# A gated linear-attention block on one NeuronCore: the decayed queries move from GpSimd to VectorE

## What is computed

```python
# attention branch: q, k, v = silu(causal_conv(xn @ W_qkv)), 8 key heads, 16 value heads of 128
q = _l2norm(repeat(q)) * 128 ** -0.5;  k = _l2norm(repeat(k))
beta = sigmoid(xn @ W_b);  g = -exp(A_log) * softplus(xn @ W_a + dt_bias)
def step(S, inp):                       # over the tokens, state S per head, 128 x 128
    S = S * exp(g_t)
    v_adj = (v_t - k_t @ S) * beta_t
    S = S + outer(k_t, v_adj)
    return S, q_t @ S
s = (rmsnorm(o) * norm_weight * silu(xn @ W_z)) @ W_out
# expert branch: the two experts with the largest summed router score, 512 -> 2048 -> 512, gelu
```

## Time and profile before

| | before |
|---|---|
| median of 3 runs | 2161.2 us (2160.35 to 2166.19) |
| profiled execution, its own time | 2165.89 us |
| span of the profiled execution | 2164.1 us |
| PE busy | 2058.8 us (95%) |
| DVE busy | 1238.0 us (57%) |
| ACT busy | 881.9 us (41%) |
| POOL busy | 966.1 us (45%) |
| `qd` on POOL (L1510) | 128 instructions, 96.1 us busy |
| mean granted clock of TensorE | 0.981 of full speed |

### The profile page before, as it was taken

The page is one execution under the profiler, slowest core; times in us unless marked ns, Lnnn a source line. Parts: engine busy times, 40 slices in busy tenths (PEclk is TensorE's granted clock), DMA queues, the critical chain, the costliest instruction groups (busy, mean ns, idle before and its releaser), DMA issues.

```text
span 2164.1 us, 39542 instructions
## 1 busy us (share of the span) xinstructions
PE 2058.8 (95%) x13994; PEld 1744.7 (81%) x13994; DVE 1238.0 (57%) x2875; ACT 881.9 (41%) x2476; POOL 966.1 (45%) x2295
## 2 busy tenths in 40 slices
PE   5479999999999999999999999999999999999999
PEld 3368888888888888888888878888888888887887
DVE  5657777777687777777776473333334433364221
ACT  2335555556465564555545432222223322232111
POOL 7276776768677776777776411001101121010001
PEclk9689999999999999999999999999999999999999
DMA  3234354434536344343434120000100111022331
GB/s 107 49 52 98 76 93 89 88 92 80 94 80 100 84 93 89 82 96 88 98 63 98 46 94 30 20 20 30 30 20 20 39 30 49 0 87 89 117 118 58
DMA packets 218996, 150.68 MB, mean 70 GB/s; under 512 B 113200, under 2 KB 200112, under 8 KB 216752
## 3 DMA queue, kind: packets, MB, share of 16 engines
q1 hardware_dynamic: 183984, 143.95, 27.9%
q10 hardware_dynamic: 34816, 4.20, 1.3%
HBM read 118.48 MB, written 29.62 MB: 68 GB/s over the span
## 4 chain that ended last, share of the span: by engine, by line
PE 56%; POOL 14%; issue 13%; DMA 8%; DVE 3%; SPq 3%; ACT 1%; ACTq 0%; POOLq 0%; DVEq 0%
PE bank L290 15%; PE bank L292 14%; PE bank L291 14%; POOL V L1530 4%; POOL prod L1528 4%; DMA VT<-v_dram 4%; PE bank L522 2%; PE bank L513 2%; DMA decb<-dec_dram 2%; PE bank L496 1%; PE bank L420 1%; PE bank L532 1%; PE bank L504 1%; POOL qd L1510 1%; POOL x_in L1484 1%
## 5 line engine op out<-in xcount | busy, mean ns | idle before, releaser
L1528 POOL TENSOR_TENSOR prod<-A_in,V 128x60 f32<-128x60 f32 (+24 forms) x992 | 295.6, 298 | 223.7 <-DMA A_in<-a_dram 158.3
L1530 POOL TENSOR_TENSOR V<-V,prod 128x60 f32<-128x60 f32 (+24 forms) x992 | 301.9, 304 | 77.7
L1584 POOL TENSOR_TENSOR ffn_w_lo<-ffn_raw,ffn_w_hi 128x1024 fp32r<-128x1024 f32 x32 | 76.7, 2398 | 497.3 <-ACT ffn_w_hi L1009 497.3
L1019 ACT ACTIVATE hid<-bank,bias 128x512 f32<-128x512 f32 x128 | 88.0, 687 | 467.2 <-PE bank L292 467.2
L1386 DVE TENSOR_TENSOR h_lo<-hid,h_hi 128x512 fp32r<-128x512 f32 x128 | 90.1, 707 | 314.3 <-ACT h_hi L1026 314.3
L1399 DVE SCALAR_TENSOR_TENSOR gate_acc<-bank,rw,gate_acc 128x512 f32<-128x512 f32 x256 | 190.4, 749 | 76.6 <-PE bank L292 69.9
L290 PE MATMUL bank<-ffn_w_hi,h_hi 128*128 128x512 f32 x512 | 202.7, 396 | 6.0 <-DVE gate_acc L1399 5.0
L290 PE MATMUL bank<-xn_hi,ffn_w_hi 128*128 128x512 f32 x512 | 202.1, 395 | 0.0
L292 PE MATMUL bank<-ffn_w_hi,h_lo 128*128 128x512 f32 x512 | 201.8, 394 | 0.0
L291 PE MATMUL bank<-ffn_w_lo,h_hi 128*128 128x512 f32 x512 | 201.8, 394 | 0.0
L292 PE MATMUL bank<-xn_hi,ffn_w_lo 128*128 128x512 f32 x512 | 201.1, 393 | 0.0
(11 more groups left out here) (217 smaller groups left out, 5235.2 us busy)
## 6 DMA issues: line engine op xcount, KB each, us to landing
E<-eg_dram SPq DMA_DIRECT2D x64, 256.0 KB, 7.7
A_in<-a_dram SPq DMA_DIRECT2D x32, 512.0 KB, 3.9
decb<-dec_dram SPq DMA_DIRECT2D x128, 128.0 KB, 4.5
og_dram<-og SPq DMA_DIRECT2D x64, 256.0 KB, 2.2
ffn_raw<-w SPq DMA_DIRECT2D x32, 512.0 KB, 3.6
og_in<-og_dram SPq DMA_DIRECT2D x16, 1024.0 KB, 5.4
w_raw<-group_w SPq DMA_DIRECT2D x48, 256.0 KB, 7.7
x_in<-x SPq DMA_DIRECT2D x8, 512.0 KB, 7.0
```

The lines of the kernel that those rows point to most:

```text
L1019: act.activation(hid[:, i % 2, :], bank[i % 4][:, :], ACT.Gelu_apprx_tanh, bias=bias1[:, k, f * NF + ft:f * NF + ft + 1]).then_inc(S_["gel ...
L1528: pool.tensor_tensor(prod[:, 0:m, 0:n], column, V[:, vb, 0:m, j:j + 1].to_broadcast([P, m, n]), MUL).then_inc(S_["product"], 1)
L1530: pool.tensor_tensor(V[:, vb, 0:m, j + 1:B32], V[:, vb, 0:m, j + 1:B32], prod[:, 0:m, 0:n], ADD).then_inc(S_["solve_step"], 1)
L1584: pool.tensor_tensor(fw[m, "lo", n % 2][:, :], raw[:, i % 2, :], fw[m, "hi", n % 2][:, :].bitcast(f32), SUB).then_inc(S_["ffn_lo"], 1)
```

## The change

The function `decayed_query` moves from the GpSimd program into the VectorE program with its three waits (the load of `decb`, the queries' activation, the matmuls that read the buffer before), and the product becomes a VectorE instruction. On VectorE the four `next_query(i)` stand right behind `chain_R(st-2, i)`; on GpSimd they are gone. Everything else keeps its place.

```diff
@@ vector
+            def decayed_query(n):
+                b, i = n // CPS, n % CPS
+                dve.wait_ge(S_[f"dec{n % 2}"], 16 * (n // 2 + 1))
+                dve.wait_ge(S_["act_q"], b + 1)
+                if n >= 2:
+                    dve.wait_ge(S_["queries"], n - 1)
+                dve.tensor_tensor(qd[:, n % 2, :, :], twice(kqT[:, b % KQ_LIFE, i, 1, :]), decb[:, n % 2, :].rearrange("p (h t) -> p h t", h=REP), MUL).then_inc(S_["qd"], 1)
...
                 if chain:
                     chain_R(st - 2, 0)
+                next_query(0)
                 if gone:
                     variance(2 * (st - 3) + 1)
...
                 if chain:
                     chain_R(st - 2, 1)
+                next_query(1)
                 if turned:
                     convolve(st - 1, "v1")
...
                     chain_R(st - 2, 2)
+                next_query(2)
...
                     chain_R(st - 2, 3)
+                next_query(3)
@@ gpsimd
-            def decayed_query(n):
...
-                next_query(0)
+
                 if gone:
                     factor(2 * (st - 3) + 1)
                 if turned:
                     eliminate(st - 1, 20, 28)
 
-                next_query(1)
                 if turned:
                     eliminate(st - 1, 28, SOLVES)
-                next_query(2)
...
                 if now:
                     eliminate(st, 8, 12)
 
-                next_query(3)
```

More of the change, by code:

```diff
@@ L1315, in attention_step, with next_query @@
                 ahead, now, turned, chain, gone = is_block(st + 1), is_block(st), is_block(st - 1), is_block(st - 2), is_block(st - 3)
+                def next_query(i):
+                    n = CPS * (st - 2) + i + 1
+                    if 0 <= n < NCHUNK:
+                        decayed_query(n)
                 if now:
@@ L1350, in attention_step @@
                     chain_R(st - 2, 2)
+                next_query(2)
+                if chain:
                     variance(2 * (st - 2))
```

## The result

The changed kernel takes **2157.72 us** (median of 22 runs, 2147.51 to 2170.15); the kernel before, run beside it, 2164.16 (22 runs). The ratio is **0.9974, with a 95% interval of 0.9961 to 0.9986**: 5.6 us less. A second comparison, in the last set of experiments, gave 2157.86 against 2162.41, 0.998 [0.9961, 0.9998]. The forecast was 1.0 us more. So the change gains a little, about the 0.3% that a measurement of this kernel can tell, and the sign of the sum was wrong.

The account below looks back on a forecast made before the run. PE was taken as the bound in the attention steps; +13.0 (chunk 1), -8.9 (L522), -1.6 (L463) and -1.5 (factor) gave +1.0 us on 2161.2, so 2162.2 us, no change (chance 0.47), range 2148 to 2174.

Parts of the forecast that it names:

- 31 steps x 0.42 = +13.0: Chunk 1: the product delays v1's convolution and so PE's z projection by 0.42 us in each of 31 steps, +13.0 us.
- in the ordinary steps it is worth next to nothing: GpSimd's relief in steps not behind a key head's change: one product gained (0.58 us), the length of VectorE's lost.
- L463's waits: PE waiting for VectorE's diagonal, 10.9 us: four places in steps 6, 10, 20 and 22 shrink by 0.42, -1.6 us.
- L522's term: PE waiting for U, mostly in steps behind a key head's change: GpSimd ends sooner, -8.9 of 9.8 us.
- two signs of being wrong: Chunk 1's L513 to L290 distance growing under 0.2 us (faster), or waits for U staying near 7 us (slower).
- What bounds it: Attention steps: PE is the bound, 196.78 of 200 us busy, waiting at v1's convolution, U and the diagonal.
- GpSimd is slowed by it: 0.2.: GpSimd's rounds lose 0.2 us to each 256-column VectorE product, some 15 to 25 us of busy time.
- VectorE waits for the factor, -1.5.: VectorE waits for GpSimd's factor, 17.0 us in 12 places; in two or three late steps it reaches PE, -1.5 us.
- `next_query(0)`, (2), (3): hidden.: These VectorE products cost PE nothing, covered by waits for L420 (1.76 us), for a DMA and for PE.
- slower rival: The relief does not reach PE: GpSimd's factor waits for the delayed variance; 2170 us, 2173 with 0.55 a product; chance 0.31.
- GpSimd's loop was the real bound: Faster rival: waits at L522 (9.8 us) and L463 (10.9) go altogether, plus 5.1 us of clock; 2147 us, chance 0.22.
- The product does not lengthen VectorE's path: Work ahead on VectorE gets quicker by as much, so +13.0 falls away, 2150 us; counted in the 0.22 chance.

Follow-up runs that it names:

- late-steps versions: Kernel before with only next_query(3) of steps 4, 8, ... and next_query(0), (1) of steps 5, 9, ... moved to VectorE, in three orders: 2151.19, 2150.96, 2156.98 us.

## Why the prediction was wrong, step by step

The forecast was +1.0 us, and the kernel got 5.6 us faster. The mechanism on PE's side was right; the terms were mis-sized, all the large ones to the same side. **The steps that failed are "31 steps x 0.42 = +13.0" (10.7 measured) and "in the ordinary steps it is worth next to nothing", by which L463's waits were put at -1.6 (-3.4 measured).** L522's term was 1.1 us short as well. Neither of the two signs of being wrong that the text names came up (a chunk-1 distance grown by under 0.2 us, waits for U near 7): they asked for a broken mechanism, and what failed were sizes.

- **What bounds it** (PE; the closed path through v1's convolution; U behind the last round; the diagonal). Right. The late product in chunk 1 took 10.4 us of PE's distances away and the doubled one added 18.8, at that place.
- **"31 steps x 0.42 = +13.0."** Mechanism right, size too large: +10.7, which is 0.34 a step. (The text's own parts, 0.424 - 0.08 + 0.1, make 0.44 and not 0.42.) The product takes 416 ns (median; 424 with GpSimd quiet) and hands over after 0.33 us, in nearly every step. That is the lower bound of the text, the one without a collision. I had added 0.1 for collisions from `w_lo_q`; in chunk 1 GpSimd is in its rounds in 30 of 31 steps, and it is the rounds that give way.
- **"GpSimd is slowed by it: 0.2."** Somewhat too large, and inside the 15 to 25 us that were given. GpSimd's busy time fell by 71.5 us where 96.1 us of products were taken off, but those overlapped their neighbours: without them the kernel before has 878.4 us of busy time, the changed one 894.6, so 16.2 came back. It is in the rounds, which took 597.5 us before and 614.6 after: 17.1 / 128 = 0.13 us a product. In step 16 the round under the product takes 0.33 us where the same round took 0.22. The Trainium skill (SBUF — State Buffer, section Who interferes with whom) calls contention for the shared ports an exclusive lock, and the prediction read this as GpSimd giving back a product's whole length. The trace agrees as to the kind and not as to the size: only 35.4 of the products' 55.6 us lie beside a busy GpSimd, and the rounds grew by half of that.
- **"L522's waits -8.9."** The last round came 1.16 us sooner in the late steps (1.1 forecast), and the wait went altogether: -10.0. I had kept back 0.2 us for a variance stuck behind the split, and capped the rest by the 9.8 us of the waits view, which misses short waits (11.1 us by the starts in the first trace, 9.0 in the second). 1.1 us too small.
- **"L463's waits -1.6."** -3.4, with a scatter of 3 us between traces of one kernel. The sentence that failed is "in the ordinary steps it is worth next to nothing": there too the last round came sooner, by 0.3 us in the mean of steps 3 to 30 (12.05 to 11.73, and 11.96 to 11.67). The text set the product that GpSimd loses behind the factor against the length of the one that delays the variance; but the factor starts only 0.1 us later (at 3.1 us of the step, 3.0 before). By kind of step the account is further off than the sum: over the floor of 0.33 us a place, the waits at L463 fell in the ordinary steps from 4.8 and 6.9 us to 1.1 and 1.7, 4.5 less in the mean, and rose in the late ones from 5.2 and 6.5 to 7.7 and 6.1, 1.0 more, where the text had none. In steps 6, 10, 20 and 22 the last round 0.3 us sooner and PE 0.33 later would make 2.6 of the 4.5; what lies between the last round and the diagonal for the rest I did not follow.
- **"VectorE waits for the factor, -1.5."** L292 to L496 gave -1.3. Right; the wait at `og` fell from 17.0 to 3.6 us.
- **"`next_query(0)`, (2), (3): hidden."** Nearly: +0.8 us. The cover of chunk 0 was read in step 16, an ordinary one, and isn't there in the late steps; doubling the three made 6.9 us of such waits in its trace.
- The sum of the waits is -3.2 where the text had +1.0: **no term had the wrong sign, and the three errors of 1 us or more are to the same side** (2.3, 1.8 and 1.1 us). 13 and 12 us nearly cancel, so errors of 10 to 20% in the two large terms are enough to decide the sign, and L463 was off by a factor of two besides. The traces add 3.4 us of clock, by chance as far as the runs tell. So of the 4.6 to 6.4 us between the medians the waits explain 3.2, and 1 to 3 us stay open.

The slower rival's 0.55 us a product, put into all its terms, makes +11 and not +12. Of the rivals, "GpSimd's loop was the real bound" asked for the last round to come over 2 us sooner: it was 1.2, and most of L463's waits stayed. Of "the relief does not reach PE" the mechanism is real: the factor now waits for the variance in every step (63.1 us, had 22.8), and this swallowed part of the relief. It didn't swallow enough: in the late steps the factor starts at 4.39 us of the step (mean) where it started at 5.03, since GpSimd's own queue of a split and a product had held it even longer. "The product does not lengthen VectorE's path" is refuted by the distance in chunk 1.

## What to carry to other kernels

When work moves between two engines of which neither is the bound, look at where it is put: behind the instruction that hands over to the bound engine it cost little here, ahead of it it cost its full pitch (the 0.33 us to the next instruction's start) in every iteration. Two lines of order were worth about as much by the medians (6.5 us) as the move itself (4.6 to 6.4). Check a cover in the iterations that are special as well as in a plain one, and where gains and prices of 10 us cancel, forecast the two sides and give the sign little weight.

## What was unexpected of the hardware

- A product of 128x256 on VectorE with two SBUF inputs lost nothing to GpSimd's short rounds (412 ns mean in chunk 1, 30 of 31 overlapped), while a round under it went from 0.22 to 0.33 us. The long split on GpSimd (1.27 us) is another matter: four-column instructions of VectorE beside it took 0.99 and 1.21 us, each to the end of the split. In both pairs the long instruction kept its time and the short one gave way, but the long one had also started first in both. The run with chunk 1's product late tells a little more. There the product itself starts beside a split of 1.28 us that is already running, ten times, and each time it ends 0.28 us behind the split (653.12 + 1.11 in the rows above, with the split's end at 653.95); it takes 0.78 to 1.39 us. The one split that started while the product ran, at 398.46, took 1.48 us. So there the later of the two gave way, whichever it was.
- VectorE's scans became quicker with the products off GpSimd: a mean of 766 and 748 ns in the two traces before, 707 and 706 after, and 735 or 736 in the three late-steps versions, which leave 104 of the 128 products on GpSimd. It is 5 to 8 us over the 128 scans, and they stayed hidden.
